# Where VectorE takes the routing pieces of a batch: in front of the slot's softmax work or behind it

## What is computed

```
x = x + tanh(g_xattn[0]) * L0_xattn(layernorm(x), ctx, ...)   # 16 heads of 64, softmax over 375 keys
x = x + tanh(g_ffn[0])   * L0_ffn(layernorm(x), ...)          # a mix by Fourier weights, one 256x256 matrix here
x = x + tanh(g_xattn[1]) * L1_xattn(layernorm(x), ctx, ctx)   # one head of 256
x = x + tanh(g_ffn[1])   * L1_ffn(layernorm(x), ...)          # 16 experts, each token takes 4

g = einsum('bth,eh->bte', t, gate_w) + gate_b                 # inside L1_ffn
vals, idx = top_k(g, 4)
w = softmax(vals)
route = sum(one_hot(idx, 16) * w)                             # then 16 experts, each weighted by its route
```

## Time and profile before

| | before |
|---|---|
| median of 3 runs | 1106.21 us (1103.28 to 1108.82) |
| profiled execution, its span | 1134.4 us |
| its time apart from the span | none is given |
| PE matmuls busy | 1039.8 us (92%) |
| weight loads busy | 957.5 us (84%) |
| DVE busy | 813.1 us (72%) |
| ACT busy | 716.6 us (63%) |
| POOL busy | 521.5 us (46%) |
| mean granted TensorE clock | 0.980 |

### The profile page before, as it was taken

One profiled execution on the slowest core, in us unless ns is written; L12 is line 12 of the kernel. 1 busy time (PEld: TensorE's weight loads), 2 busy tenths in 40 slices (PEclk: granted clock), 3 DMA queues, 4 the chain that ended last, 5 costly groups with the idle time before them and its releaser, 6 DMA issues. The chain is left out here.

```text
span 1134.4 us, 22413 instructions
## 1 busy us (share of the span) xinstructions
PE 1039.8 (92%) x7055; PEld 957.5 (84%) x7055; DVE 813.1 (72%) x2017; ACT 716.6 (63%) x1853; POOL 521.5 (46%) x747
## 2 busy tenths in 40 slices
PE   4899999999999999999999999999998778859995
PEld 4899898989889988889898988898897767858993
DVE  4656786868777787878686878677876865846665
ACT  4645766676766767676767676676766545635661
POOL 5413245445454635454545445463534225544441
PEclk9999999999999999999999999999998889989999
DMA  6332122222323232222222222212213522344469
GB/s 175 99 110 59 43 57 65 56 63 59 78 56 81 53 79 65 69 61 61 64 54 70 60 53 58 64 50 62 54 46 93 180 62 89 116 111 156 135 191 315
DMA packets 77569, 98.47 MB, mean 87 GB/s; under 512 B 14459, under 2 KB 69373, under 8 KB 77200
## 3 DMA queue, kind: packets, MB, share of 16 engines
q1 hardware_dynamic: 68064, 79.04, 26.3%
q0 software_dynamic: 8848, 16.96, 4.3%
q10 hardware_dynamic: 544, 1.05, 0.3%
HBM read 44.08 MB, written 23.03 MB: 59 GB/s over the span
## 5 line engine op out<-in xcount | busy, mean ns | idle before, releaser
L935 POOL TENSOR_TENSOR prob<-prob,rinv 112x750 f32<-112x750 f32 x128 | 184.1, 1438 | 250.3 <-DVE rinv L1609 239.8
L1027 ACT ACTIVATE prob<-ps_s,negmax 112x375 f32<-112x375 f32 x256 | 143.9, 570 | 61.5 <-DVE negmax L1603 52.4
L1616 DVE TENSOR_TENSOR pT_lo<-ps_pt,pT_hi 125x672 fp32r<-125x672 f32 x128 | 108.5, 847 | 63.1 <-ACT pT_hi L1164 57.7
L1707 PE MATMUL ps_kv<-ctxT_hi,wkv 128*128 128x376 f32 x512 | 138.5, 351 | 2.1 <-DVE v_lo L1276 1.4
L1603 DVE TENSOR_REDUCE negmax<-ps_s 112x2 f32<-112x750 f32 x128 | 119.0, 930 | 1.6 <-PE ps_s L1955 1.5
L1707 PE MATMUL ps_kv<-wkv,ctxT_hi 128*125 128x512 f32 x384 | 110.7, 410 | 2.4 <-DVE k_low L1272 2.4
L1017 ACT ACTIVATE v_hi<-ps_kv 125x512 fp32r<-125x512 f32 x96 | 57.3, 597 | 80.9 <-PE ps_kv L1707 75.8
L894 POOL DMA_INDIRECT places<-ysb,place_i x72 | 70.9, 984 | 81.1 <-issue 43.0
L1965 PE MATMUL ps_pt<-ident,prob 112*125 112x112 f32 x768 | 104.4, 272 | 2.3 <-POOL prob L935 2.3
L1164 ACT ACTIVATE pT_hi<-ps_pt 125x672 fp32r<-125x672 f32 x128 | 93.6, 731 | 5.7 <-PE ps_pt L1965 1.1
L1965 PEld LDWEIGHTS ps_pt<-ident,prob 112*125 112x125 f32 x768 | 94.8, 190 | 2.6 <-POOL prob L935 2.5
(11 more groups left out here) (312 smaller groups left out, 2752.8 us busy)
## 6 DMA issues: line engine op xcount, KB each, us to landing
kx<-k_low SPq DMA_DIRECT2D x256, 94.0 KB
xg<-rows_by_expert SPq DMA_DIRECT2D x72, 128.0 KB
qx_hi<-qx_hi SPq DMA_DIRECT2D x64, 112.0 KB, 2.2
zb<-places SPq DMA_DIRECT2D x16, 448.0 KB, 15.7
ctx_in<-in_ctx SPq DMA_DIRECT2D x16, 375.0 KB
stage_w<-in_L_ffn_mlp_w SPq DMA_DIRECT2D x16, 256.0 KB, 5.3
arena<-in_L_ffn_mlp_w SPq DMA_DIRECT2D x16, 256.0 KB, 5.8
stage_w<-in_L_xattn_w_kv SPq DMA_DIRECT2D x4, 512.0 KB, 11.9
```

The lines of the kernel that those rows point to most:

```text
L935: e_prob.done(eng.tensor_tensor(prob[0:TQ, p % 2, :, :], prob[0:TQ, p % 2, :, :], rinv[:, 2 * p:2 * p + 2].unsqueeze(2).broadcast_to([TQ, ...
L1027: e_exp.done(eng.activation(prob[0:TQ, p % 2, half, :], S[0:TQ, half, 0:SK], ACT.Exp, bias=negmax[:, h:h + 1], accum_out=rowsum[:, h:h + 1]))
L1616: e_pt_lo.done(eng.tensor_tensor(pT_lo[:, :, :, :].rearrange("p h k t -> p h (k t)"), PT[0:KEYT, :, 0:NKEY * TQ], pT_hi[:, :, :, :].bitcas ...
L1707: last = eng.matmul(out_, lhs(i, k), rhs(j, k), start=(n == 1), stop=(n == KT * len(PASSES)))
```

## The change

The routing pieces leave `tail_first` and become a function of their own, `gate_first`, which DVE calls behind `pT_lo` of the slot and in front of the slot's groups. Nothing else is touched, and no engine but DVE has another order.

```
@@ -1327,6 +1327,8 @@
                                                         kbq[:, k:k + 1], qk_hi[:, k, :].bitcast(F32),
                                                         ALU.add, ALU.subtract)
                     e_tl_dve.done(last)
+            def gate_first(g):
+
                 tb = also(g, 35, 34)
                 if tb:
 
@@ -1618,6 +1620,7 @@
                             PT[0:KEYT, :, 0:NKEY * TQ],
                             pT_hi[:, :, :, :].bitcast(F32).rearrange("p h k t -> p h (k t)"),
                             ALU.subtract))
+                gate_first(g)
                 for step, kind, n in kv_groups(g):
                     projection(step, kind, n)
                 for k in SLOT_TILES.get(g - LAST_BODY, ())[:1]:
```

## The result

| | before | after |
|---|---|---|
| median of 4 runs | 1104.74 us (1101.27 to 1108.82) | 1117.32 us (1116.38 to 1119.56) |
| ratio, 95% interval | | 1.0093 [1.006, 1.0126] |
| profiled execution: its time, its span | span 1134.4 us | 1116.81 us, span 1115.1 us |
| mean granted TensorE clock | 0.980 | 0.982 |

The change costs 0.93% by the ratio of the runs, 6.6 to 13.9 us by its interval; the two medians stand 12.6 us apart. The ratio is taken within one level.

A forecast was written before the change was run, and what follows sets the result against it. PE was taken as the bound, waiting little more than 1 us a batch. Stalls at route (0.5) and the norm (0.27 more), taken as 0.78 a place, times 14 gave 10.9 us: 1117.1 us, 1.0% slower, range 1110 to 1123.

The forecast's parts named there:

- The uncovered waits: DVE, swapped slot: rinv waits 0.34 us for ACT, pT_lo 0.99; DVE 1.52 us late behind the pieces.
- gl and the output projection: PE's output projection load: gl ends at 2.52 against the load at 2.81, 0.29 us early, hidden.
- route: PE's load of route: first stall, about 0.5 us a place, passing to what is queued behind it.
- The norm: DVE's chain from x to n12t: 0.77 us late, passed on to PE in full; 0.78 taken a place.
- rival (c): DVE clears the slot sooner: 14 x 0.44 = 6.2 us gained, 1100 us; chance 0.05.
- The gain side: rinv 2.1 us earlier, so POOL's product and pT_lo end earlier; neither was waited for, gain 0.
- POOL beside DVE: POOL's product would lie at 0.7 to 2.1, ahead of the pieces at 2.35, blocking none; cost 0.
- The distance in the trace of after: From one slot 35 to the next: 53.6 us instead of 52.80.
- Absorbed (b): Lateness absorbed by PE waits whose releasers are not late: 1106 us, within noise; chance 0.06.
- Costlier (d): pT_hi 0.5 us later through feedback, so PE waits at gl: 7 us more, 1124; chance 0.06.
- (a): L1290 gets in front of POOL's L819 in the norm: 0.39 us a place, 5.5 us, 1111.7; chance 0.08.
- Carrying 10.9 us over from a span of 1134.4 to a median of 1106: Whole kernel: the 10.9 us of stalls, read in the profiled execution, added unscaled to the median of 1106.21.

The follow-up runs named there:

- the last experiment: The kernel before, with POOL's copy of xb1 (L819) put behind the slot's product instead of in front: ratio 0.9999 [0.9978, 1.0019].
- the repeat: The changed kernel, unchanged, run again later in another group: 1141.86 us against 1132.5 for the kernel before, ratio 1.0082.

## Why the prediction was right

- **The uncovered waits.** Forecast 0.34 and 0.99, found 0.35 and 0.99; `qx_lo` forecast 1.52 late, found 1.53. The order with four pieces in front shows that it is the cover that counts, not the order as such.
- **gl and the output projection.** Forecast 0.29 us of room, hidden. `gl` ends at 409.13 and its reader loads at 409.41 with no idle time in front: hidden.
- **route.** Forecast a stall of about 0.5, 14 times; found 7.5 us in 14 waits, the longest 0.5. One detail was off. The prediction let the 0.5 pass on to everything behind; 0.29 passed on, since the next load (L1754) stood 0.21 behind the load of `route` without a wait (415.02 to 415.23 above) and stands beside it with one (414.00 and 414.00). It changed no sum, because the norm's lateness swallowed both.
- **The norm.** Forecast `x` and `n12t` 0.77 late, passed on in full, 0.78 a place. Found 0.78 on PE in the trace of after. The distance grew by 0.70 at the level where both kernels have a trace, 9.8 us in 14 places, 0.86% of 1136; the ratios measured are 1.0093 and 1.0082. So by these distances a tenth was given back behind the norm; the mean distances and the spread of the ratios leave this open. One reading of the prediction was wrong: that `n12t` was already what PE waits for, by 0.13. Only its weight load waited. With `n12t` 0.46 earlier the matmul started where it had (the last experiment), so the 0.13 that rival (c) counted as a gain isn't there. The lateness still passes on in full, since the two arrive together.
- **The gain side.** Forecast 0 for the earlier `rinv`. The order that gives it up and keeps the wait takes 53.67 against 53.50; DVE was 0.08 later there, so the gain is 0.1 to 0.2 a place at most, and its ratio doesn't differ clear of noise.
- **POOL beside DVE, costed at 0.** Right for this order: with `pT_lo` in between, POOL's product (407.28, 1.44 us long) was over at 408.72, before the pieces began at 408.97. It is right by 0.25 us only, or by 0.53 if it is counted to the first piece with two on-chip inputs, at 409.25 (`gl` takes one from PSUM, the bank memory that PE writes, and the maximum has a single input). Without `pT_lo` in between the same product falls on a comparison and costs 1.20.
- **The distance in the trace of after.** Forecast 53.6, found 52.40 (408.97 to 461.37). Not a failure of a term: the forecast started from 52.80, which belongs to the other level. At that level it is 53.50.
- **The rivals.** Absorbed (b) and faster (c) are out by the ratio; (c) needed an earlier `pT_hi`, and it came at the same place. Costlier (d) needed `gl` to be waited for, and it isn't. The lucky order of L1290 and L819 (a) did not happen: L1290 took 0.69. (The paragraph on POOL in the prediction calls it the second rival; it is the first of the list.)
- **Carrying 10.9 us over from a span of 1134.4 to a median of 1106.** The prediction had an argument for this and no measurement: the trace that it read was at the higher level and the median at the lower. It held. The ratio gives 10.3 us (6.6 to 13.9), the medians 12.6.

## What to carry to other kernels

Work without a dependence in front of an instruction that waits is cover; before moving it, read from a place without it how long the wait is, and subtract the idle time that the next links have, here 0.75 to 0.78 us of a 1.53 us lateness. Stalls of one late engine on another don't add up: the last reader's lateness is the price. A reordering also moves what the other engine starts at that moment, and a GpSimd instruction that is released just ahead of a DVE instruction with two on-chip inputs can cost as much as a long wait: 1.20 us here.

## What the runs showed of the hardware

**Blocking by POOL's read.** The 16x16 comparison on DVE: 0.41 us alone, 1.61 beside a 1.44 us multiplication on POOL that began 0.11 earlier. The one-column L1290: 0.22 alone, 0.68 to 0.69 beside a 0.73 us addition. The delay follows what is left of the POOL instruction when DVE's begins: 1.33 us left and 1.20 lost at the comparison (413.59, product over at 414.92), 0.67 left and 0.46 lost at L1290 before. The one ended 0.28, the other 0.01 behind POOL's. `pT_lo` and `qx_lo`, which take one input from PSUM, kept their durations beside the same product.

**Two levels of one kernel.** The kernel before ran at 1101 to 1109 us in one group of runs and at 1129 to 1146 in the others, at granted clocks that don't differ (after: 0.982 and 0.980). The record names three different chips for the three later groups and none for the first, so whether the level goes with the chip is open. The kernel after has a trace at each level, with spans of 1115.1 and 1141.0, so they can be laid side by side. Taken from `gl`, the starts on PE, DVE, ACT and POOL agree within 0.02 us for 26 us. Then ACT, at the higher level (trace of the repeat):

```profile
438.80 0.21 ACT L1027 ACTIVATION_READ_ACCUMULATOR prob<-ps_s,negmax 112x1 f32 x1
439.93 0.53 ACT L1151 ACTIVATE oT<-ps_ot 64x112 f32<-64x112 f32 x2 [0.92 <-PE ps_ot L2001]
```

```profile
438.80 0.50 PE L2001 MATMUL ps_ot<-pT_hi,v_lo 125*128 125x224 f32 x3
...
441.93 0.54 PE L1788 MATMUL ps_kv<-ident,ctx_in 125*128 125x125 f32 x3 [0.79 <-ACT xnT L996]
```

and at the lower one:

```profile
434.91 0.21 ACT L1027 ACTIVATION_READ_ACCUMULATOR prob<-ps_s,negmax 112x1 f32 x1
435.45 0.53 ACT L1151 ACTIVATE oT<-ps_ot 64x112 f32<-64x112 f32 x2 [0.33 <-PE ps_ot L2001]
```

```profile
434.92 0.50 PE L2001 MATMUL ps_ot<-pT_hi,v_lo 125*128 125x224 f32 x3
```

The matmul that `oT` reads ends at 439.30 and at 435.42. ACT starts 0.63 us behind it in the one and 0.03 in the other, with its earlier work done in both. PE waits for what follows on ACT (`xnT`), and has lost 0.47 us. A second place follows 7 us later (`qx_hi`, L1010, which waits 0.52 for PE's queries in the one and not at all in the other), and by the end of the batch they make 1.1 us, 52.40 against 53.50 a batch. What holds ACT back there is not in the trace, and stays open; nothing of it depends on the change, whose ratio is the same at both levels within its intervals.
